# Layer norms begun in the stage before them, and a shifted norm whose statistics are taken inside local attention

## What is computed

```python
def _layernorm(x, axis=-1, eps=1e-05):
    m = jnp.mean(x, axis=axis, keepdims=True)
    v = jnp.var(x, axis=axis, keepdims=True)
    return (x - m) / jnp.sqrt(v + eps)

for l in range(4):
    x = x + tanh(g_xattn[l]) * xattn[l](_layernorm(x), ctx)
    x = x + tanh(g_ffn[l])   * ffn[l](_layernorm(x))
# xattn: joint attention | cross-attention with an inner norm (gamma, beta) | linear attention
#        | a dense gelu product over the context tokens
# ffn:   8 experts, one per token | 16 experts, 4 per token, and 2 shared, SwiGLU
#        | two layers of local attention | SwiGLU with fake-quantised nvfp4 factors

# one of the two layers of local attention (8 heads of 64, windows of 128 tokens)
h = shift_token(x)          # second half of the features comes from the token before
q, k, v = split(h @ wqkv); q, k = l2norm, scale, rotary
x = x + local_attention(q, k, v) @ wo       # a window sees itself and the one before
h = shift_token(x)
h = (h - mean(h)) / sqrt(var(h) + 1e-05) * lg + lb
a, g = split(h @ w1 + b1)                   # 256 -> 2 x 682
x = x + (a * gelu(g)) @ w2 + b2
```

## Time and profile before

| | |
|---|---|
| median of 3 runs | 2498.22 us (2495.98 to 2506.04) |
| profiled execution | 2497.99 us beside a span of 2495.7 us |
| mean granted TensorE clock | 0.905 of full speed |
| TensorE busy | 2052.7 us, 82% of the span, 14744 products |
| VectorE busy | 1759.9 us, 71%, 3778 instructions |
| ScalarE busy | 1327.8 us, 53%, 3064 instructions |
| GpSimd busy | 1045.6 us, 42%, 1053 instructions |
| DMA | 80.81 MB in 29257 packets, 32 GB/s on average |

### The profile page before, as it was taken

How to read it: one execution, slowest core, us unless ns; L and a number is a source line. 1 busy time by engine, 2 the same in 40 slices (tenths; PEclk the granted TensorE clock), 3 DMA queues, 4 the chain that set the end, 5 groups by cost and what they waited for, 6 DMA issues and landing times. The chain is left out here.

```text
span 2495.7 us, 41249 instructions
## 1 busy us (share of the span) xinstructions
PE 2052.7 (82%) x14744; PEld 1486.0 (60%) x14744; DVE 1759.9 (71%) x3778; ACT 1327.8 (53%) x3064; POOL 1045.6 (42%) x1053
## 2 busy tenths in 40 slices
PE   6899999966589997799997879886998886985254
PEld 5444444456556665688886668675877775764122
DVE  6899999855655554776765676766666675668896
ACT  4488888834354443333332247473436564323797
POOL 1333233115543431455553654543535452422554
PEclk9899999988799998899998989998998988987586
DMA  4244344154300001100002000002000001000000
GB/s 110 33 55 50 48 54 54 23 217 126 57 1 1 1 1 81 51 1 1 1 1 87 1 1 2 1 2 95 1 1 1 1 1 38 1 35 25 0 1 34
DMA packets 29257, 80.81 MB, mean 32 GB/s; under 512 B 6016, under 2 KB 20096, under 8 KB 27392
## 3 DMA queue, kind: packets, MB, share of 16 engines
q0 software_dynamic: 11136, 22.38, 7.2%
q1 hardware_dynamic: 17920, 55.80, 6.5%
HBM read 45.07 MB, written 12.06 MB: 23 GB/s over the span
## 5 line engine op out<-in xcount | busy, mean ns | idle before, releaser
L3028 ACT ACTIVATE probs<-psum 128x512 f32<-128x512 f32 (+1 forms) x640 | 344.0, 601 | 91.7 <-PE psum L2952 76.4
L3070 DVE TENSOR_REDUCE max_parts<-psum 128x1 f32<-128x512 f32 x512 | 320.1, 685 | 26.3 <-PE psum L2890 20.5
L199 PE MATMUL psum<-x_upper,weights_upper 128*128 128x512 f32 (+2 forms) x556 | 220.8, 397 | 27.5 <-POOL weights_rest L211 12.9
L211 POOL TENSOR_TENSOR weights_rest<-L1f,weights_upper 128x256 fp32r<-128x256 f32 x216 | 179.6, 858 | 147.9 <-ACT weights_upper L341 147.9
L2952 PE MATMUL psum<-q_stack,k_stack 50*128 50x512 f32 (+1 forms) x640 | 235.4, 453 | 0.2 <-ACT probs L3028 0.2
L199 PE MATMUL psum<-x_rest,weights_upper 128*128 128x512 f32 (+2 forms) x556 | 217.4, 391 | 0.0
L199 PE MATMUL psum<-x_upper,weights_rest 128*128 128x512 f32 (+2 forms) x556 | 216.3, 389 | 0.0
L2890 PE MATMUL psum<-k_stack,q_stack 48*128 48x512 f32 x512 | 192.6, 465 | 12.5 <-ACT probs L3028 7.8
L2962 PE MATMUL psum<-probs,v_tok 128*17 128x256 f32 x2560 | 194.7, 386 | 0.2 <-ACT probs L3028 0.2
L199 PE MATMUL psum<-weights_upper,hidden_upper 128*128 128x256 f32 (+1 forms) x572 | 178.2, 312 | 5.2 <-DVE hidden_rest L211 2.7
L2526 POOL TENSOR_TENSOR probs<-probs,row_sum 128x1024 f32<-128x1024 f32 x64 | 121.0, 1894 | 138.5 <-DVE row_sum L2545 138.5
(11 more groups left out here) (515 smaller groups left out, 6035.0 us busy)
## 6 DMA issues: line engine op xcount, KB each, us to landing
k_stack<-k_parts POOLq DMA_DIRECT2D x56, 147.2 KB, 3.8
L1f<-in_L1f SPq DMA_DIRECT2D x1, 6016.0 KB
L2f<-in_L2f SPq DMA_DIRECT2D x2, 2268.0 KB, 9.8
L1x<-in_L1x SPq DMA_DIRECT2D x1, 4226.0 KB
k_stack<-k_parts POOLq DMA_DIRECT2D x56, 73.6 KB, 4.1
L0f<-in_L0f SPq DMA_DIRECT2D x1, 4096.0 KB, 12.3
L2a<-in_L2a SPq DMA_DIRECT2D x2, 2048.0 KB, 11.4
slots_x<-zeros SPq DMA_DIRECT2D x1, 3840.0 KB, 13.3
```

Source lines behind the costliest of these rows:

```text
L199: ins = pe.matmul(out, lhsT(a).bitcast(F32R), rhs(b).bitcast(F32R), start=start and n == 0, stop=stop and n == len(PASSES) - 1, skip_group ...
L211: return engine.tensor_tensor(dst.bitcast(F32R), src, up_part, ALU.subtract)
L3028: act.activation(pb[0:m, n % NPB, (1 - e) * 512:(2 - e) * 512], net.ps[0:m, ST + (2 * n + e) % NS, :], ACT.Exp, scale=HD ** -0.5)\
L3070: ins = v.tensor_reduce(mx3[:, u % 2, a + 4 * e, k:k + 1], src, AX.X, ALU.max)
```

## The change

- `RowStats` gets tiles for variance, root, inverse, minus mean times inverse, and for statistics of half rows (`both`, whose 12 entries per tile are set once to the count of 64 by a memset in the first local layer, and `later`).
- One turned memory `norm_turned` of [128, 2, 2048] fp32 is kept through the kernel. It holds each norm's output in place of the stages' own `xT`; before a tile is turned, its normalised rows lie in the same 128 columns (`in_turned`). Local attention's values and the shifted norm's half rows `xn` lie in it too, and the quantised stage's `ratio` lies elsewhere.
- A new class `NormAhead` holds the pieces of a norm, and the stage before issues them for the tiles that are already final: the cross-attention stage for 12 tiles of its inner norm and 8 of the routed feed-forward's at its last block, the routed feed-forward for 12 tiles of linear attention's norm, linear attention for 12 tiles of the norm into `y_tok`, the second `local_ffn` for 12 of the last feed-forward's. In a feed-forward the root for group g-1 stands in unit 2 of group g, and ScalarE's tiles in unit 3.
- `norm_end` is the block behind the barrier. It takes the last four tiles' statistics, root, inverse and rows while TensorE turns the first twelve; VectorE takes one of the eight copies. At the end of the feed-forwards `RowStats.take` is left out for the last group.
- Cross-attention's wq_rest and one small constant go from GpSimd to VectorE; the copies of four tail values go from VectorE to ScalarE.
- The shifted norm's bn_stats leave that block. `local_attend` takes both halves' statistics of window t-3 (`halves_of`) behind `add_y` of window t-2, and those left at the pass's end; one of four first-half tiles is normalised by ScalarE (`SHARED`).

```diff
+    def halves(self, v, step, y, t):
+
+        H2 = D // 2
+        step(v.bn_stats(self.later[:, t, :], y[:, t, H2:D]))
+        step(v.bn_stats(self.both[:, t, 0:6], y[:, t, 0:H2]))
...
+class NormAhead:
+    def __init__(self, net, ctx, src, place, again=False):
+        self.net, self.src, self.place, self.again = net, src, place, again
+        self.var_ready, self.sd_ready, self.rs_ready, self.rows_ready, self.normed = [
+            net.sem(ctx, f"ahead_{name}") for name in ("var", "sd", "rs", "rows", "normed")]
+    def spread(self, v, lo, hi):
+        r = self.net.rows
+        if self.again:
+            ins = v.tensor_scalar(r.ve[:, lo:hi], r.mv[:, lo:hi, 1], 1.0 + EPS, EPS * EPS, ALU.mult, ALU.add)
+        else:
+            ins = v.tensor_scalar(r.ve[:, lo:hi], r.mv[:, lo:hi, 1], EPS, None, ALU.add)
+        ins.then_inc(self.var_ready, 1)
+    def root(self, act, part, lo, hi):
+        r = self.net.rows
+        act.wait_ge(self.var_ready, part + 1)
+        act.activation(r.sd[:, lo:hi], r.ve[:, lo:hi], ACT.Sqrt).then_inc(self.sd_ready, 1)
+    def invert(self, v, part, lo, hi):
+        r = self.net.rows
+        v.wait_ge(self.sd_ready, part + 1)
+        v.reciprocal(r.rs[:, lo:hi], r.sd[:, lo:hi]).then_inc(self.rs_ready, 1)
+        v.wait_ge(self.rs_ready, part + 1)
+        v.scalar_tensor_tensor(r.nb[:, lo:hi], r.mv[:, lo:hi, 0], -1.0, r.rs[:, lo:hi], ALU.mult, ALU.mult)\
+            .then_inc(self.rows_ready, 1)
+    def vector(self, v, tiles):
+        r = self.net.rows
+        for t in tiles:
+            dst, own = self.place(t)
+            v.tensor_scalar(dst, own(self.src), r.mv[:, t, 0:1], r.rs[:, t:t + 1], ALU.subtract, ALU.mult)\
+                .then_inc(self.normed, 1)
+    def scalar(self, act, part, tiles):
+        r = self.net.rows
+        act.wait_ge(self.rows_ready, part + 1)
+        for t in tiles:
+            dst, own = self.place(t)
+            act.activation(dst, own(self.src), ACT.Identity, bias=r.nb[:, t:t + 1], scale=r.rs[:, t:t + 1])\
+                .then_inc(self.normed, 1)
...
+def norm_end(net, ahead, parts, turns=None, xT=None, gain=None, shift=None, after=None):
+    nc = net.nc
+    LO = T - GT
+    OWN, OTHER = [(LO, LO + 1, LO + 2), (LO + 3,)] if turns else [(LO, LO + 1), (LO + 2, LO + 3)]
+    BY_VECTOR = (G - 1) * C
+    with ExitStack() as ctx:
+        vec = net.sem(ctx, "end_vec")
+        early = net.sem(ctx, "turned")
+        block = ctx.enter_context(nc.Block())
+        out = lambda n: xT[:, n % C, n // C * GN:(n // C + 1) * GN]
+        @block.vector
+        def _(v):
+            step = Steps(v, vec)
+            net.rows.take(v, step, ahead.src, range(LO, T))
+            step.settle()
+            ahead.spread(v, LO, T)
+            ahead.invert(v, parts, LO, T)
+            ahead.vector(v, OWN)
+            if turns:
+                if after is not None:
+                    v.wait_ge(after.landed, 16)
+                v.wait_ge(early, BY_VECTOR + 1)
+                c = BY_VECTOR % C
+                if gain is None:
+                    v.tensor_copy(out(BY_VECTOR), net.ps[:, BY_VECTOR, :])
+                else:
+                    v.tensor_scalar(out(BY_VECTOR), net.ps[:, BY_VECTOR, :], gain[:, c:c + 1], shift[:, c:c + 1],
+                                    ALU.mult, ALU.add)
+        if turns:
+            @block.tensor
+            def _(pe):
+                for n in range(G * C):
+                    g, c = divmod(n, C)
+                    if n == BY_VECTOR:
+                        pe.wait_ge(ahead.normed, T)
+                    for t in range(g * GT, (g + 1) * GT):
+                        ins = pe.transpose(net.ps[:, n, t % GT * P:(t % GT + 1) * P], turns(t, c), net.ident[:])
+                    ins.then_inc(early, 1)
+        @block.scalar
+        def _(act):
+            def take(n):
+                c = n % C
+                act.wait_ge(early, n + 1)
+                if gain is None:
+                    act.copy(out(n), net.ps[:, n, :])
+                else:
+                    act.activation(out(n), net.ps[:, n, :], ACT.Identity, bias=shift[:, c:c + 1], scale=gain[:, c:c + 1])
+            if turns:
+                if after is not None:
+                    act.wait_ge(after.landed, 16)
+                take(0)
+                take(1)
+            ahead.root(act, parts, LO, T)
+            if turns:
+                take(2)
+            ahead.scalar(act, parts, OTHER)
+            if turns:
+                for n in range(3, G * C):
+                    if n != BY_VECTOR:
+                        take(n)
...
+                if ahead is not None and g >= 1 and u == 2:
+                    ahead.root(act, g - 1, (g - 1) * GT, g * GT)
+                if ahead is not None and g >= 1 and u == 3:
+                    ahead.scalar(act, g - 1, range((g - 1) * GT, g * GT))
...
+                if ahead is not None and g == G - 1:
+                    return
                 net.rows.take(v, step, y if then is None else x, range(g * GT, (g + 1) * GT))
+                if ahead is not None:
+                    step.settle()
+                    ahead.spread(v, g * GT, (g + 1) * GT)
...
+                if ahead is not None and g >= 1 and u == 2:
+                    ahead.invert(v, g - 1, (g - 1) * GT, g * GT)
...
+            ahead.root(act, 0, 0, T - GT)
+            ahead.scalar(act, 0, range(GT, T - GT))
...
+            step.settle()
+            ahead.spread(v, 0, T - GT)
+            ahead.invert(v, 0, 0, T - GT)
+            ahead.vector(v, range(GT))
             for k in (PAIRS - 2, PAIRS - 1):
                 add_y(k)
-                statistics(k)
...
+                act.wait_ge(cleared, 1)
+                tail_value(2)
+                tail_value(3)
+                for g in range(G - 1):
+                    ahead.root(act, g, g * GT, (g + 1) * GT)
+                    if g == 0:
+                        tail_value(6)
+                        tail_value(7)
+                    ahead.scalar(act, g, range(g * GT, (g + 1) * GT))
...
-                pool.wait_ge(wq_upper, 1)
-                rest(pool, wq[1][:], w("wq"), wq[0][:])
-                pool.tensor_scalar(gbo[:], w("bo"), factor, None, ALU.mult)
...
+                value(0)
+                value(1)
+                rows_of(0)
+                v.wait_ge(wo_upper, 1)
+                rest(v, wo[1][:], w("wo"), wo[0][:])
+                ahead.invert(v, 0, 0, GT)
+                value(4)
+                value(5)
+                v.wait_ge(wq_upper, 1)
+                rest(v, wq[1][:], w("wq"), wq[0][:])
+                v.tensor_scalar(gbo[:], w("bo"), factor, None, ALU.mult)
+                rows_of(1)
+                ahead.invert(v, 1, GT, 2 * GT)
+                rows_of(2)
+                ahead.invert(v, 2, 2 * GT, 3 * GT)
+                v.wait_ge(gathered[G - 1], 16 * GT)
+
+        norm_end(net, ahead, G - 1, lambda t, c: nT[:, c, t * P:(t + 1) * P], nT, gain=w("gain"), shift=w("shift"))
...
+                        if d == 0 and u == U:
+                            net.rows.root_table(act)
...
-                net.rows.root_table(act)
+                then.root(act, 0, 0, T - GT)
+                then.scalar(act, 0, range(GT, T - GT))
...
+                        if u == U + 1 and d == 0:
+                            then.invert(v, 0, 0, T - GT)
+                            then.vector(v, range(GT))
...
+                        if u == U and d == 1:
+                            step.settle()
+                            then.spread(v, 0, T - GT)
...
-            pe.wait_ge(own_ready, 1)
             dst = net.ps[:, 0, MOVED:MOVED + T * 6]
             pe.matmul(dst, net.down, flat(own[:]), start=True, stop=False, skip_group_check=True)
...
-                pe.wait_ge(half_ready[c], GT * (g + 1))
+                pe.wait_ge(half_ready[c], (GT - 1 if c == 0 else GT) * (g + 1))
+                if c == 0:
+                    pe.wait_ge(shared_ready, g + 1)
...
-            step(v.memset(st[:], float(H2 // 2)))
-            for t in range(T):
-                ins = v.bn_stats(own[:, t, :], y[:, t, H2:D])
-            ins.then_inc(own_ready, 1)
-            step.settle()
-            for t in range(T):
-                step(v.bn_stats(st[:, t, 0:6], y[:, t, 0:H2]))
             v.wait_ge(moved, 1)
...
+            v.scalar_tensor_tensor(nb[:], mr[:, :, 0], -1.0, mr[:, :, 1], ALU.mult, ALU.mult).then_inc(nb_ready, 1)
             for t in range(T):
-                v.tensor_scalar(xn[:, t, 0:H2], y[:, t, 0:H2], mr[:, t, 0:1], mr[:, t, 1:2], ALU.subtract,
-                                ALU.mult).then_inc(half_ready[0], 1)
+                if t not in SHARED:
+                    v.tensor_scalar(xn[:, t, 0:H2], y[:, t, 0:H2], mr[:, t, 0:1], mr[:, t, 1:2], ALU.subtract,
+                                    ALU.mult).then_inc(half_ready[0], 1)
...
+            act.wait_ge(nb_ready, 1)
+            for t in SHARED:
```

(31 more changed lines are left out.)

133 lines of the change are left out of this document (73 added, 60 removed).

## The result

Before 2498.30 us, median of 7 runs; after 2484.30 us, median of 7 (2477.92 to 2489.86). The medians lie 14.0 us apart. The ratio is 0.9935, 95% interval 0.9919 to 0.9952, which is 16 us less (12 to 20), where 16.8 were forecast. The profiled execution took 2480.42 us beside a span of 2478.6 us; the span is 17.1 us shorter. The sum came out nearly right, but not each of its terms.

The account below looks back on a forecast made before the run. It took the time as the sum of stages between barriers, each set by the engine arriving last. Terms -12.6 - 4.9 + 0.1 - 9.9 + 9.1 + 1.4 = -16.8 from 2498.0 gave 2481.2 us, range 2473 to 2490.

Parts of the forecast that it names:

- Plain barriers: Barriers into routed feed-forward, linear attention and last feed-forward: TensorE bounds the norm behind them, 4.2 us less each, -12.6 us.
- Cross-attention's k/v stage: Stage end before cross-attention's inner norm: ends with the gather's last landing, norm from 678.7 to 685.8 us, -4.9 us.
- I read this as 2.0 us of blocking and charge it once more: Cross-attention's gathers: VectorE's moved wq_rest blocks one as wo_rest did, moving the last landing to about 678.4 us.
- Into the shifted norm: Shifted norm, twice: half-row statistics leave the block, but the L2f pack's landing holds the copies; 4.95 us each, -9.9 us.
- So a new wait appears, ScalarE for the DMA: Shifted norm: ScalarE's copies wait for the L2f pack, some 8.5 us after block start, and run to 14.3.
- Local attention: Four passes: statistics lengthen four windows a pass (1.5 us) and add a 0.76 us tail; 2.3 a pass, +9.1 us.
- Feed-forwards: Routed and last, three groups each: VectorE's settle and variance come where TensorE waits, +1.4 us for six (0 to 3).
- Into local attention: Linear attention's end and closing norm: block ends near 1434.1, norm takes 3.9 us against 4.99; +0.1 us (-1 to +2).
- Two of the prediction's own signs: Two gathers of some 3.5 us instead of one; prediction wrong if stages the change leaves alone grow or shrink.
- the drain that the prediction names beside its sum: Feed-forwards: by the skill a table switch costs about 2.66 us with its drain; activation 3.6 us late, sum unchanged.

## Why the prediction was right, and where not

**Plain barriers.** -12.6 foreseen, -12.4 measured (4.80, 4.16, 3.49). The mechanism is as it was put: TensorE's transposes bound the norm (5.9 us against 6.15), though with less room than foreseen: at two of the barriers the last rows were done 4.05 us after the start, as forecast, and TensorE took the first of them at 4.3 and 4.1 us, not at 4.5. The statistics are free inside it, and in front of the barrier they cost what they take and a longer time at the lower clock behind it. The L2x pack was there in time.

**Cross-attention's k/v stage.** -4.9 foreseen, -5.5 measured, but by a wrong step: "I read this as 2.0 us of blocking and charge it once more". wq_rest cost the gathers 0.34 us. The block lasts until the VectorE instruction ends and falls on a gather that begins after it has; wq_rest started 0.01 us behind a gather, which went free. By the Trainium skill (SBUF — State Buffer, "Who interferes with whom") a tensor_tensor of two SBUF operands is inferred not to hold up descriptor writing. Here a gather was held, 2.1 us in nine profiles of this schedule and 0.5 us when the subtraction was cut in four; the measurement decides. The same section lets such a tensor_tensor contend with a GpSimd instruction that reads SBUF, and a gather takes its indices from the SBUF tile `slots`, so it may be that read which is held; no run tells the two apart. VectorE's keys_rest, with one input in PSUM, held nothing: a gather that began inside it took 1.54 us. So the norm began at 677.5 instead of 678.7; it took 7.35 us, 7.1 foreseen.

**Into the shifted norm.** -9.9 foreseen, -11.2 measured between the block's start and its end (5.7 and 5.5). The step "So a new wait appears, ScalarE for the DMA" is right about the wait and was charged too much. In the second norm the arithmetic from it comes out (14.3 foreseen, 13.7 measured), but without the wait the norm ends only 0.2 us sooner (0.7 counted from VectorE's first copy). In the first the pack landed 6.9 us after the block's start and not 8.5, and there the landing sets nothing: 13.6 with it and without it. VectorE's own chain, which I had put at 6.0 us of gain, gave 5.7 and 6.2 and ends the norm or stands right behind what does.

**Local attention.** +9.1 foreseen, +8.2 measured: 4 x 1.06 in the windows (1.5 each foreseen) and 3.9 in four tails (0.76 each foreseen; 0.78 in front of a pass, 1.1 and 1.2 in front of a shifted norm). A statistics pair of 0.39 us lengthened the turn by 0.27; where it stands, some of it is hidden. In front of a shifted norm only 0.78 us of the tail are the statistics: with them taken back into the norm the gap was still 0.35 and 0.41 us longer than before the change, and what makes that isn't shown.

**Feed-forwards.** +1.4 foreseen, about +1.0 measured: 0.7 in the routed one, where TensorE's waits for VectorE went from 1.0 to 1.7 us, and 0.3 in the local one, from 2.6 to 2.8. ScalarE's root and tiles cost nothing.

**Into local attention.** +0.1 foreseen, +0.1 measured.

**What wasn't foreseen** adds to +6.7 and -3.6 us, and the terms that were sized came out 3.1 lower in all, so that it doesn't show in the sum. Cross-attention's end lost 2.7 us: there I had priced nothing, though the change puts a variance, a root and twelve tiles there, and the statistics that stood there already became what TensorE waits for once its products weren't slow. With the same code and the clock falling as before, 0.3 to 0.4 us of it remained. The routing lost 0.9 us, for a reason that stands in the trace of the changed kernel:

```profile
1000.68 0.61 DVE L1026 TENSOR_SCALAR pair<-pair 128x64 f32<-128x64 f32 x1
1001.33 0.89 DVE L1027 TENSOR_TENSOR masked_scores<-masked_scores,pair 128x256 f32<-128x256 f32 x1
...
1005.09 0.83 DVE L1031 TENSOR_TENSOR keys_of_order<-keys_of_order,const 128x256 f32<-128x256 f32 x1
...
1000.47 2.33 POOL L347 TENSOR_TENSOR weights_rest<-L1f,weights_upper 128x256 fp32r<-128x256 f32 x3 [1.76 <-ACT weights_upper L478]
...
1003.18 2.46 POOL L347 TENSOR_TENSOR weights_rest<-L1f,weights_upper 128x256 fp32r<-128x256 f32 x3 [0.39 <-ACT weights_upper L478]
```

Three VectorE instructions took 0.61, 0.89 and 0.83 us where they took 0.20, 0.43 and 0.43 before: they meet GpSimd's remainders. That is this execution's doing and not the change's. In the second profile of the same kernel GpSimd came later against them, and they took their old times (the second of them and GpSimd's remainders):

```profile
1002.58 0.42 DVE L1027 TENSOR_TENSOR masked_scores<-masked_scores,pair 128x256 f32<-128x256 f32 x1
...
1003.30 2.29 POOL L347 TENSOR_TENSOR weights_rest<-L1f,weights_upper 128x256 fp32r<-128x256 f32 x3 [2.93 <-ACT weights_upper L478]
```

From ScalarE's table load to the end of this stretch it was 18.8 to 18.9 us in ten of the twelve profiles of the changed kernel and its variants, as before the change, and 19.6 in the two that have the long instructions. Stretches at the lower clock cost 1.5 us ahead of pass 1 and 1.6 ahead of pass 4; the first of these isn't bound to the change, for in four of the other kernels, whose code is the same there, that stretch took 175.6 us, as foreseen. And the last two stretches gave 2.1 and 1.5 us beyond the barrier's 3.5. The last one was 104.0 to 104.7 us in ten of twelve profiles of the changed kernel and its variants, 106.0 and 106.5 in two, 105.9 before; what made it so stays open.

So the time was right because each term that was sized lay within 1.3 us of what it measured, and because the rest cancelled, which is luck. Two of the prediction's own signs went against it: there was one gather of 3.5 us or more and not two, and stretches that the change leaves alone did shrink.

## What to carry to other kernels

A barrier between stages is worth what stands on both sides of it: move the norm's early tiles in front and its last statistics behind, and look which engine then bounds it. Work put into a loop's ring costs by its place, not by its length: the same 0.39 us cost 0.27 us a turn behind an addition and nothing ahead of a wait that was longer. Price each edit against the stage's next bound as well (a wait that shows in the timeline may have another one right behind it), and compare stages, not total times, where the difference is a few us.

## What the runs showed of the hardware

- A VectorE subtraction of two SBUF operands and GpSimd's indirect DMA exclude each other for the length of one instruction: 3.65 us for a gather that begins 0.05 us behind it, 1.55 for one that begins 0.03 us behind it, 2.07 when the subtraction is cut in four. The gathers read their indices from SBUF, and whether that read or the writing is what is held stays open. The other way round a VectorE instruction of 0.16 us stood for 5.77 and ended with a GpSimd subtraction of 5.10 us.
- The same untouched stage took from 641.5 to 651.9 us in thirteen profiles, with TensorE's granted clock at the 1.2 GHz level for 65 to 89 us of it.
- Behind the same schedule the lower level falls mostly at the same places; a shift of a few us by an edit lets it fall on other products, worth 3.4 us and more in a stretch that the edit doesn't touch (197.6 to 197.9 us in three kernels, 200.6 to 202.3 in the other ten profiles).
- A table load took 1.28 us each time, four of them in a row of small activations as well, with no gap of more than 0.02 us around these four; the drain that the prediction names beside its sum doesn't show in these rows.
